# The half chunk of layers 1 and 2 laid out over all 128 partitions, and layer 2's moved to seventh place

## The reference: what is computed

```python
for i, f in enumerate([128, 128, 128]):
    h = prev.shape[1]                      # 39, then 64, then 64
    Wr = Ws[i].reshape(h, M, f)
    z = relu(einsum('bhk,bmk,hmf->bfk', prev, x0, Wr) + bs[i][None, :, None])
    half = f // 2
    results.append(z[:, :half])            # to the output
    prev = z[:, half:]                     # 64 channels to the next layer
pooled = sum(concatenate(results, axis=1), axis=-1)
return pooled @ W_lin
```

## Time and profile before

| | |
|---|---|
| median of three runs | 1971.02 us |
| profiled execution, its own time | 1970.57 us |
| its span, first to last instruction | 1968.6 us |
| PE busy | 1962.8 us |
| VectorE busy | 1912.1 us |
| ScalarE busy | 586.7 us |
| GpSimd busy | 154.5 us |
| granted TensorE clock | 1.000 (2.4 GHz) |

### The profile page before, as it was taken

One profiled execution on the slowest core, in us unless ns is written; L12 is line 12 of the kernel. 1 busy time (PEld: TensorE's weight loads), 2 busy tenths in 40 slices (PEclk: granted clock), 3 DMA queues, 4 the chain that ended last, 5 costly groups with the idle time before them and its releaser, 6 DMA issues.

```text
span 1968.6 us, 29931 instructions
## 1 busy us (share of the span) xinstructions
PE 1962.8 (100%) x10304; PEld 739.1 (38%) x10304; DVE 1912.1 (97%) x1445; ACT 586.7 (30%) x717; POOL 154.5 (8%) x186
## 2 busy tenths in 40 slices
PE   9999999999999999999999999999999999999999
PEld 3333343333333333333343333333333333333333
DVE  8989999999999999999999999999999999999988
ACT  2333223332133322333222332223332133322332
POOL 1001000010100100001000010010100100000000
DMA  7999988788977889778798777987778977789720
GB/s 179 189 194 186 188 174 169 162 171 175 191 165 158 175 167 199 168 154 175 159 207 169 154 173 162 195 183 157 168 159 183 192 160 166 164 175 197 149 43 1
DMA packets 122523, 327.45 MB, mean 166 GB/s; under 512 B 24529, under 2 KB 43370, under 8 KB 122501
## 3 DMA queue, kind: packets, MB, share of 16 engines
q1 hardware_dynamic: 97539, 303.05, 71.2%
q0 software_dynamic: 24192, 23.87, 7.8%
q10 hardware_dynamic: 770, 0.23, 0.1%
HBM read 303.11 MB, written 0.01 MB: 154 GB/s over the span
## 4 chain that ended last, share of the span: by engine, by line
PE 97%; DVE 2%; DMA 0%; issue 0%; ACT 0%; ACTq 0%; DVEq 0%
PE acc L845 37%; PE acc L722 23%; PE acc L921 20%; PE acc L850 11%; PE acc L910 2%; PE acc L714 2%; DVE prod L408 1%; PE acc L789 1%; PE acc L935 1%; PE acc L928 1%; DMA bias<-b 0%; DVE prod L414 0%; PE acc L729 0%; ACT prev L1043 0%; ACTq L1141 0%
## 5 line engine op out<-in xcount | busy, mean ns | idle before, releaser
L408 DVE TENSOR_TENSOR prod<-prev,x_bc 128x2048 f32<-128x2048 f32 x511 | 1139.7, 2283 | 11.1 <-PE acc L722 9.4
L845 PE MATMUL acc<-prod,w_sb 128*64 128x512 f32 x3360 | 748.4, 593 | 0.0
L921 PE MATMUL acc<-prod,w_sb 128*64 128x512 f32 x1064 | 462.4, 593 | 0.1
L845 PEld LDWEIGHTS acc<-prod,w_sb 128*64 128x64 f32 x3360 | 237.3, 137 | 442.4 <-issue 391.4
L928 PE MATMUL acc<-prod,w_sb 128*64 128x512 f32 x840 | 384.3, 593 | 0.0
L722 PE MATMUL acc<-x_rot,w_sb 128*64 128x512 f32 x1240 | 277.5, 593 | 0.0
L1090 ACT ACTIVATE diff<-acc 64x256 f32<-64x256 f32 x56 | 21.3, 380 | 735.3 <-PE acc L850 735.0
L921 PEld LDWEIGHTS acc<-prod,w_sb 128*64 128x64 f32 x1064 | 143.9, 137 | 248.3 <-issue 193.5
L414 DVE TENSOR_TENSOR prod<-prev,x_bc 128x1024 f32<-128x1024 f32 x193 | 230.0, 1218 | 1.5
L381 DVE TENSOR_TENSOR x_rot<-x_rot,x_rep 128x1024 f32<-128x1024 f32 (+1 forms) x186 | 214.5, 1222 | 1.3 <-issue 0.3
L1014 ACT ACTIVATE prev<-acc,bias 32x1024 f32<-32x1024 f32 x140 | 155.1, 1108 | 3.1 <-DVE prod L408 0.9
(11 more groups left out here) (100 smaller groups left out, 1246.7 us busy)
## 6 DMA issues: line engine op xcount, KB each, us to landing
x_bc<-x SPq DMA_DIRECT2D x312, 256.0 KB, 15.5
x_bc<-x SPq DMA_DIRECT2D x156, 512.0 KB, 21.4
x_rot<-x SPq DMA_DIRECT2D x155, 312.0 KB
x_rot<-x SPq DMA_DIRECT2D x217, 156.0 KB
x_bc<-x SPq DMA_DIRECT2D x124, 128.0 KB, 11.0
x_rep<-x SPq DMA_DIRECT2D x62, 192.0 KB
x_bc<-x_bc POOLq DMA_DIRECT2D x56, 128.0 KB, 10.1
x_rot<-x SPq DMA_DIRECT2D x124, 44.0 KB
```

The source lines that it names most:

```text
L408: mul = nc.vector.tensor_tensor(prod[:, s:s + w, :], twice, x_bc[:, u, t:t + w, :], ALU.mult)
L845: mm = nc.tensor.matmul(acc1[f, h, :], w[:, f], prod[:, s, BANK * h:BANK * h + BANK], start=False, stop=stop, skip_group_check=closed)
L921: nc.tensor.matmul(acc2[0:HALF, u, :], w, prod[:, s, 0:BANK], start=(pos == 1), stop=False)
```

## The change

The half chunk takes a layout of its own: columns 0 to 511 on one half of the partitions and 512 to 1023 on the other (for u = 1 the halves are swapped). Its field is loaded in that layout into `x_t1` (two DMAs of 64 x 512 in place of one of 128 x 1024), and ScalarE writes the 64 channels in that layout into `prev_t1` (two more instructions of 64 x 512 per layer and block, one of 128 x 512 in block 0's layer 1). VectorE's product becomes one instruction of 128 x 512 in both layers. PE does as many matmuls of the same sizes as before, with the partition halves taken in another order where u = 1, and in `layer2_left`. In layer 2 the half chunk is no longer made first: `RUNS2` puts it in seventh place, behind run (10,1). For the last block it stays first (`RUNS_END`).

```diff
+    T1_AT = 6
+    RUNS2 = [*RUNS[1:T1_AT + 1], RUNS[0], *RUNS[T1_AT + 1:]]
...
             def load_bc_t1(i, u, loaded):
 
-                src = rows_of(i, M - 1, [[0, P], [1, NB]])
-                sp.dma_start(x_bc[:, u, T1, :], src).then_inc(loaded, 16)
+                for h in range(NH):
+                    k = HALF * (h ^ u)
+                    src = rows_of(i, M - 1, [[0, HALF], [1, BANK]], BANK * h)
+                    sp.dma_start(x_t1[k:k + HALF, u, :], src).then_inc(loaded, 16)
...
-                if layer == 2 and t == T1:
-                    k = slice(HALF * u, HALF * u + HALF)
-                    mul = nc.vector.tensor_tensor(left2[k, :], old[k, :], new[k, :], ALU.mult)
+                old = prev[layer - 1][a]
+                if t == T1:
+                    to = left2[:, u, :] if layer == 2 else prod[:, s, 0:BANK]
+                    mul = nc.vector.tensor_tensor(to, prev_t1[layer - 1][:], x_t1[:, u, :], ALU.mult)
...
-                elif t == T1:
-                    for h in range(NH):
-                        k, cols = slice(HALF * h, HALF * h + HALF), slice(BANK * h, BANK * h + BANK)
-                        mul = nc.vector.tensor_tensor(prod[k, s, cols], old[k, cols], new[k, cols], ALU.mult)
...
             def products2(i, u, first, part=range(NR), last=False, phase=CH):
 
-                runs = RUNS_END if last else RUNS
+                runs = RUNS_END if last else RUNS2
...
-                    elif pos in (0, 11):
-                        dve.wait_ge(prev_ready[1], i * 2 + (1 if pos == 0 else 2))
+                    elif pos in (0, 1, 11):
+                        dve.wait_ge(prev_ready[1], i * 2 + (1 if pos == 1 else 2))
...
             def layer2_left(first=None):
                 for u in range(U):
-                    k = slice(HALF * u, HALF * u + HALF)
                     for h in range(NH):
-                        mm = nc.tensor.matmul(acc2[HALF * h:HALF * h + HALF, u, :], w2_sb[k, CH - 1, :],
-                                              left2[k, BANK * h:BANK * h + BANK],
+                        k = slice(HALF * (h ^ u), HALF * (h ^ u) + HALF)
+                        mm = nc.tensor.matmul(acc2[HALF * h:HALF * h + HALF, u, :], w2_sb[k, CH - 1, :], left2[k, u, :],
                                               start=(u == first), stop=(u != first))
...
+            def spread_t1(h, acc, layer, u):
+                k = slice(HALF * (h ^ u), HALF * (h ^ u) + HALF)
+                return nc.scalar.activation(prev_t1[layer][k, :], acc[HALF:P, h, :], ACT.Relu,
+                                            bias=bias[HALF:P, layer:layer + 1])
...
                 act.sem_inc(prev_ready[0], 1)
+                nc.scalar.activation(prev_t1[0][:], acc_state, ACT.Relu, bias=bias[:, 3:4])
...
                     if h == 1:
                         op.then_inc(prev_ready[1], 1)
+                    spread_t1(h, acc1, 1, a)
...
-                for g, done in ((1, left_half_ready), (0, prev_ready[1])):
-                    nc.scalar.activation(prev[1][0][HALF * g:HALF * g + HALF, :], src, ACT.Relu,
-                                         bias=bias[HALF:P, 1:2]).then_inc(done, 1)
+                for h in range(NH):
+                    op = spread_t1(h, acc1, 1, 1)
+                op.then_inc(left_half_ready, 1)
+                for g in range(2):
+                    op = nc.scalar.activation(prev[1][0][HALF * g:HALF * g + HALF, :], src, ACT.Relu, bias=bias[HALF:P, 1:2])
+                op.then_inc(prev_ready[1], 1)
```

More of the change, by code:

```diff
@@ L45, in cin_kernel @@
     RUN_OF = [n for n, (_, w) in enumerate(RUNS) for _ in range(w)]
+    T1_AT = 6
+    RUNS2 = [*RUNS[1:T1_AT + 1], RUNS[0], *RUNS[T1_AT + 1:]]
+    RUN_OF2 = [next(n for n, (p, w) in enumerate(RUNS2) if p <= pos < p + w) for pos in range(CH)]
     NR = len(RUNS)
@@ L71, in cin_kernel @@
     BC_T1, BC_T2 = len(XB_GROUPS), len(XB_GROUPS) + 1
-    BC_LOADS = [QPT] * len(XB_GROUPS) + [1, 2]
+    BC_LOADS = [QPT] * len(XB_GROUPS) + [2, 2]
     SMALL = 6
@@ L121, in cin_kernel @@
         x_rot_s = sb("x_rot_s", [P, BANK])
-        x_bc = sb("x_bc", [P, U, T + 2, NB])
+        x_bc = sb("x_bc", [P, U, T + 1, NB])
+        x_t1 = sb("x_t1", [P, U, BANK])
         prev = [[sb(f"prev{l}{a}", [P, NB]) for a in range(2)] for l in (1, 2)]
+        prev_t1 = [sb(f"prev_t1{l}", [P, BANK]) for l in (1, 2)]
         prod = sb("prod", [P, RING, NB])
@@ L140, in cin_kernel @@
         pool = sb("pool", [P, BATCH])
-        left2 = sb("left2", [P, NB])
+        left2 = sb("left2", [P, U, BANK])
         wl1_all = sb("wl1_all", [P, QUAD])
@@ L401, in product @@
                 s = (phase + pos) % RING
-                old, new = prev[layer - 1][a], x_bc[:, u, t, :]
-                if layer == 2 and t == T1:
-                    k = slice(HALF * u, HALF * u + HALF)
-                    mul = nc.vector.tensor_tensor(left2[k, :], old[k, :], new[k, :], ALU.mult)
+                old = prev[layer - 1][a]
+                if t == T1:
+                    to = left2[:, u, :] if layer == 2 else prod[:, s, 0:BANK]
+                    mul = nc.vector.tensor_tensor(to, prev_t1[layer - 1][:], x_t1[:, u, :], ALU.mult)
                 elif w == 2:
@@ L408, in product @@
                     mul = nc.vector.tensor_tensor(prod[:, s:s + w, :], twice, x_bc[:, u, t:t + w, :], ALU.mult)
-                elif t == T1:
-                    for h in range(NH):
-                        k, cols = slice(HALF * h, HALF * h + HALF), slice(BANK * h, BANK * h + BANK)
-                        mul = nc.vector.tensor_tensor(prod[k, s, cols], old[k, cols], new[k, cols], ALU.mult)
                 else:
-                    mul = nc.vector.tensor_tensor(prod[:, s, :], old[:], new, ALU.mult)
+                    mul = nc.vector.tensor_tensor(prod[:, s, :], old[:], x_bc[:, u, t, :], ALU.mult)
                 mul.then_inc(prod_ready, 1)
@@ L432, in products1_seeded @@
                     if n in (9, 11):
-                        dve.wait_ge(first_bc_loaded[0 if n == 9 else 1], 32 if n == 9 else 16)
+                        dve.wait_ge(first_bc_loaded[0 if n == 9 else 1], 32)
                     if n == 3:
@@ L526, in products2 @@
                         dve.wait_ge(left_half_ready, 1)
-                    elif last and pos == 1:
-                        dve.wait_ge(prev_ready[1], i * 2 + 1)
-                    elif pos in (0, 11):
-                        dve.wait_ge(prev_ready[1], i * 2 + (1 if pos == 0 else 2))
+                    elif pos in (0, 1, 11):
+                        dve.wait_ge(prev_ready[1], i * 2 + (1 if pos == 1 else 2))
                     if pos > 0:
@@ L707, in _, with split @@
         def _(pe):
-            def split(acc, w, rhs, start, stop):
+            def split(acc, w, s, u, start, stop):
                 for h in range(NH):
-                    k = slice(HALF * h, HALF * h + HALF)
+                    k = slice(HALF * (h ^ u), HALF * (h ^ u) + HALF)
                     for o in range(2):
                         f = slice(HALF * o, HALF * o + HALF)
-                        mm = nc.tensor.matmul(acc[f, h, :], w[k, f], rhs[h], start=start, stop=stop)
+                        mm = nc.tensor.matmul(acc[f, h, :], w[k, f], prod[k, s, 0:BANK], start=start, stop=stop)
                 return mm
@@ L822, in layer1_first, with layer1 @@
                         pe.sem_inc(left_asked, 1)
-                        split(acc1, w1_sb[:, c, :], [prod[0:HALF, s, 0:BANK], prod[HALF:P, s, BANK:NB]],
-                              False, True).then_inc(chunk_used, 1)
-            def layer1(i, runs, phase=0, ahead=None, run_of=RUN_OF):
+                        split(acc1, w1_sb[:, c, :], s, 0, False, True).then_inc(chunk_used, 1)
+            def layer1(i, u, runs, phase=0, ahead=None, run_of=RUN_OF):
                 pe.wait_ge(res01_ready, i * 2 + 1)
@@ L832, in layer1 @@
                         pe.sem_inc(left_asked, 1)
[L833 to L834 removed]
+                        split(acc1, w1_sb[:, c, :], s, u, True, False).then_inc(chunk_used, 1)
                         if ahead is not None:
@@ L882, in layer1_paired @@
                 pe.sem_inc(left_asked, 1)
-                split(acc1, w1_sb[:, c, :], [prod[0:HALF, 0, 0:BANK], prod[HALF:P, 0, BANK:NB]],
-                      True, False).then_inc(chunk_used, 1)
+                split(acc1, w1_sb[:, c, :], 0, u, True, False).then_inc(chunk_used, 1)
                 pe.wait_ge(res01_ready, i * 2 + 2)
@@ L902, in layer1_paired, with layer2 @@
                     layer0_left(range(U), ahead)
-            def layer2(i, u, runs, part=range(1, CH), opened=False, run_of=RUN_OF, phase=CH):
+            def layer2(i, u, runs, part=range(1, CH), opened=False, run_of=RUN_OF2, phase=CH):
                 if part[0] == 1 and not opened:
@@ L919, in layer2_paired @@
                     w, s = w2_sb[:, ORDER[pos], :], (CH + pos) % RING
-                    pe.wait_ge(prod_ready, runs + RUN_OF[pos] + 1)
```

(24 more changed lines are left out.)

## The result

The changed kernel takes **1983.51 us**, median of six runs (1982.98 to 1983.67), against 1971.03 us for the kernel before in six (1970.1 to 1972.3). The ratio is 1.0063, 95% interval 1.0053 to 1.0074: slower by 12.5 us. The forecast was 1984.5 us.

A forecast was written before the change was run, and what follows sets the result against it. PE was taken as the bound, VectorE following with 1.9 us of air a step. The loop's 12.7 us plus 1.2 for head, blocks 0 and 1 and tail gave +13.9 on 1970.57: 1984.5 us, range 1980 to 1988.5.

The forecast's parts named there:

- The bound and the cap: Loop: PE bounds; in layer 2 the ring holds VectorE's run (8,2) until PE ends position 1, leaving 0.09 us margin.
- The price of a block's stall: Layer 2, position 18: PE starts at s (layer 2's start on PE) + 15.11, wanting s + 14.59; 0.57 us with restart.
- The loop: 14 steps, each 1.14 us of new stalls less 0.23 us of old stalls gone: 12.7 us slower.
- Head and blocks 0 and 1: Block 0's layer 1: extra ScalarE copy ahead of run (4,2), +0.7 us; layer 2 stalls in blocks 0 and 1, +1.1.
- Layer 1's half chunk: VectorE's 1.41 us become 0.61, so PE's 0.16 us at run (2,2) of layer 1 goes.
- ScalarE: Extra 0.69 us copy ahead of run (1,1)'s event: with u = 0 VectorE waits 0.4 us, 0.6 of cover, cost nothing.
- The sign that VectorE would be idle for 1 to 2 us before run (8,2): Layer 2 in the changed profile: VectorE idle 1 to 2 us before that run, the idle time ended by PE.
- PE's order of quarters: `layer2_left`, 8 instructions in 1.09 us: new order takes the same four array quarters, so it is free.
- rival C: Much slower: new quarter order makes PE take two at a time, 28 x 0.86 = 24 us more, 2008; chance 0.04.
- The tail: Last block, half chunk still first: VectorE's 1.25 us become 0.61, -0.6 us.
- A: Rival, not slower: half chunk finds a gap behind run (8,2), or ring lets VectorE go further; 1967.5 us; chance 0.10.
- B: Rival, no change: the move costs less, or only one block of a step stalls; 1971 to 1976 us; chance 0.06.

The follow-up runs named there:

- experiment 7: experiment 1 with ScalarE's 128 x 512 copy of block 0 behind the turned copy, not ahead of it: 1966.80 us, ratio 0.9978 to the kernel before.
- experiment 9: experiment 7 with both ScalarE copies for layer 2's half chunk behind run (1,1)'s event in the loop: 1966.39 us, ratio 0.9976 to the kernel before.
- experiment 4: Kernel before, old layout, with its 64 x 1024 half chunk product moved to seventh place in layer 2: 2005.65 us, ratio 1.0176.
- experiment 1: Changed kernel with layer 2's half chunk in fifth place, right ahead of run (8,2), in place of seventh: 1968.03 us, ratio 0.9985 to the kernel before.
- experiment 5: Changed kernel with the half chunk in the new layout but first in layer 2, as before: 1975.16 us, ratio 1.0021 to the kernel before.
- experiment 8: Kernel before, old layout, with its 64 x 1024 half chunk product in fifth place of layer 2: 1968.90 us, ratio 0.9990.

## Why the prediction was right, point by point

**The bound and the cap.** Right. PE's stalls are where the prediction put them, ended by VectorE. That the ring is the cap is shown three ways: the price appears between fifth and sixth place, is gone with two slots more, and grows with the product's length.

**The price of a block's stall**, 0.57 us predicted: position 18 starts at 1004.90, s + 15.11, to the hundredth as predicted, and the product's 0.61 us was right. By distances, 0.44 and 0.05 at position 18 and 0.05 at position 16, a restart that the prediction did not have, make 0.54.

**The loop**, 12.7 us predicted. Layer 0 of block 3 starts at 182.41 us before and 184.10 now; that of block 30 at 1822.97 and 1836.07. That is 11.4 us over 27 of the 28 stalls, and 11.9 with the last one. Too high by 0.8 for two reasons. A step grew by 0.87 and not by 0.91 (two stalls of 0.54 less 0.21 of relief), which makes 0.6. And in the kernel before, the first step was 0.25 longer than the others (0.70 us ahead of position 18, from 206.71 to 207.41, where the others have 0.45), so more came back there: I read one step and multiplied.

**Head and blocks 0 and 1**, 0.7 and 1.1 predicted. Run (4,2) of block 0, as the earlier trace rows, and the pair of PE behind it:

```profile
30.43 2.29 DVE L415 TENSOR_TENSOR prod<-prev,x_bc 128x2048 f32<-128x2048 f32 x1 [1.01 <-ACT prev L1051]
```

```profile
32.87 1.08 PE L723 MATMUL acc<-prod,w_sb 128*64 128x512 f32 x4 [0.96 <-DVE prod L415]
```

PE waits 0.96 us where it waited 0.25 before: 0.71. It goes on at 32.87 where it was 32.21 before, 0.66, but two executions of one kernel differ by 1.1 there (experiment 7), so the two waits are the evidence. The rest of the 1.69 us up to block 3's layer 0 is 1.03.

**Layer 1's half chunk.** Right: VectorE makes it in 0.6 us (1004.76, next run 0.60 later), and PE has no stall at run (2,2) of layer 1 any more.

**ScalarE.** Right: with u = 0 its event comes late, 0.46 us in the changed kernel against 0.4 predicted, and run (8,2) still waits for PE, 0.40 us where 0.6 of cover were predicted:

```profile
1043.64 1.23 DVE L417 TENSOR_TENSOR prod<-prev,x_bc 128x1024 f32<-128x1024 f32 x1 [0.46 <-ACT prev L1109]
...
1051.87 2.29 DVE L415 TENSOR_TENSOR prod<-prev,x_bc 128x2048 f32<-128x2048 f32 x1 [0.40 <-PE acc L926]
```

The sign that VectorE would be idle for 1 to 2 us before run (8,2) holds with u = 1 (1.74) and not with u = 0. "Cost nothing" holds in seventh place. In fifth place it costs the 0.05 of experiment 9, because there the half chunk uses up the cover.

**PE's order of quarters.** Right; rival C is out. `layer2_left`, as the earlier trace rows:

```profile
1006.77 1.09 PE L933 MATMUL acc<-left,w_sb 64*64 64x512 f32 x8
...
1067.77 1.09 PE L715 MATMUL acc<-prod,w_sb 64*64 64x512 f32 x8
```

The same 1.09 us; the second row is layer 1's half chunk with u = 1, also 1.09 before (at 1059.74). The trace agrees with the Trainium skill's TensorEngine Tiling (Array Packing), Key Properties, that tiles operate independently: which quarter comes first does not matter. The switch from matmuls of 128 rows to those of 64 takes 0.53 in place of 0.43 us here (1006.24 to 1006.77). Before it is 0.55 (998.68 to 999.23), with the pair's second matmul 0.03 behind its first, where here the two start together. That is not the order either: in experiment 4, with the old order, it is 0.53 (1017.26 to 1017.79), and in experiment 1, with the new one, 0.55 (997.53 to 998.08).

**The tail**, -0.6 predicted. VectorE's half chunk of the last block, as the earlier trace rows, takes 0.60 us from start to start in place of 1.26:

```profile
1953.84 0.68 DVE L412 TENSOR_TENSOR left<-prev_t,x_t 128x512 f32<-128x512 f32 x1
1954.44 1.22 DVE L417 TENSOR_TENSOR prod<-prev,x_bc 128x1024 f32<-128x1024 f32 x1
```

From block 30's layer 0 to the end it is 145.43 us against 145.63. One stall of 0.54 (block 29) is in that, so the tail gave 0.74. PE's wait of 0.71 us is gone; of the waits that follow it in the kernel before, two of 0.26 and 0.27 are left.

**The rivals.** A's point was that the margin of 0.09 us would have to be over 0.6; experiment 1 has A's time, 1968.0, but reached by the place. B's one stall a step did not occur; both blocks stall.

Sum by rows: 1.69 + 11.41 - 0.20 = 12.9 us of span, against 13.9.

## What to carry to other kernels

Where two engines pass work through a ring, find the first instruction that the ring can stop at the start of a phase: here, time saved ahead of it was worth next to nothing, and time put behind it counted in full but for a margin of 0.09 us, since PE takes a chunk of layer 2 faster than VectorE makes one. So place an extra instruction right ahead of it, but not so early that its own wait holds the queue; here fifth against sixth place is worth 16 us, and second place is the worst of all. Compare distances between starts on the bound engine, and do it to 0.05 us, since a margin of 0.09 us decided this case.

## What the runs showed that I had not expected

A stall of PE in layer 2, however short, is followed by a start that comes 0.05 us late (0.48 in place of 0.43), even where the distance before it shows only 0.01 to 0.02 of stall (1002.69 here, and position 16 in experiment 5). And a distance of two VectorE instructions that is 0.13 us shorter, with the same instructions on both sides, went with a step 0.13 us shorter in experiment 8, 1.8 us in the loop; why the distance differs is open.
